# Cross-attention on one core: the scores' operand laid out by head, scores a slot later, input loads ahead of the copies

## What is computed

```python
Q = split_heads(query @ Wq + bq)          # x: (16, 512, 512)
K = split_heads(key @ Wk + bk)            # ctx: (16, 77, 512)
V = split_heads(value @ Wv + bv)
scores = einsum('bhqd,bhkd->bhqk', Q, K) / sqrt(32)
attn = softmax(scores, axis=-1)
ctx = einsum('bhqk,bhkd->bhqd', attn, V)
out = ctx.transpose(0, 2, 1, 3).reshape(B, S, 512) @ Wo + bo
return layer_norm(out + query, ln_gamma, ln_beta)
```

## Time and profile before

| | |
|---|---|
| three runs, median (lowest to highest) | 966.35 us (964.39 to 969.38) |
| the profiled execution | 968.15 us, span 966.4 us |
| mean granted TensorE clock | 0.82 |
| busy: PE, DVE, POOL, ACT | 71%, 57%, 47%, 38% of the span |
| DMA | 129.58 MB, mean 134 GB/s; packets took 50.4% of 16 engines' span |
| chain that ended last | SP's queue 33%, PE 26%, DVE 16%, DMA 7% |

### The profile page before, as it was taken

The page is one execution under the profiler, slowest core; times in us unless marked ns, Lnnn a source line. Parts: engine busy times, 40 slices in busy tenths (PEclk is TensorE's granted clock), DMA queues, the critical chain, the costliest instruction groups (busy, mean ns, idle before and its releaser), DMA issues.

```text
span 966.4 us, 11992 instructions
## 1 busy us (share of the span) xinstructions
PE 683.1 (71%) x3336; PEld 477.9 (49%) x3336; DVE 550.9 (57%) x971; ACT 367.8 (38%) x667; POOL 449.8 (47%) x399
## 2 busy tenths in 40 slices
PE   7987467677876666678776767678776767677773
PEld 6865235445554444445554444455554444455452
DVE  5343455665664546665655556666655556666635
ACT  5311332443444334443443334343443334344331
POOL 0411233554554445554544445554554445554458
PEclk9988678888887777888877777888777778888777
DMA  7643745445453555445453555445454655445432
GB/s 286 252 110 109 180 112 129 118 124 135 121 145 102 134 145 150 117 126 126 126 129 111 149 144 150 112 130 123 121 129 117 151 144 147 117 119 130 109 107 76
DMA packets 105680, 129.58 MB, mean 134 GB/s; under 512 B 49936, under 2 KB 49936, under 8 KB 105648
## 3 DMA queue, kind: packets, MB, share of 16 engines
q1 hardware_dynamic: 105648, 129.19, 50.4%
HBM read 53.94 MB, written 24.35 MB: 81 GB/s over the span
## 4 chain that ended last, share of the span: by engine, by line
SPq 33%; PE 26%; DVE 16%; issue 12%; DMA 7%; POOL 1%; ACT 0%; DVEq 0%; POOLq 0%
SPq L531 23%; PE p_o L660 13%; DVE part L813 6%; PE p_s L626 6%; SPq L517 4%; DMA z<-nmt 4%; DVE nmr L842 3%; DMA z<-ql 3%; PE p_a L612 3%; DVE ql L862 3%; SPq L468 2%; DVE y L802 2%; PE p_q L596 2%; SPq L490 1%; PE p_o L98 1%
## 5 line engine op out<-in xcount | busy, mean ns | idle before, releaser
L626 PE MATMUL p_s<-z,ks 97*77 97x512 f32 x256 | 116.9, 502 | 249.8 <-DMA z<-nmt 161.0
L718 ACT ACTIVATE prob<-p_s 77x512 f32<-77x512 f32 x256 | 144.3, 589 | 202.3 <-PE p_s L626 200.2
L870 DVE TENSOR_REDUCE nm<-p_a 128x4 f32<-128x308 f32 x256 | 118.9, 476 | 163.5 <-PE p_a L612 159.7
L972 POOL TENSOR_TENSOR cl<-cxt,ch 128x512 fp32r<-128x512 f32 x64 | 82.8, 1293 | 229.8 <-ACT ch L743 229.8
L626 PEld LDWEIGHTS p_s<-z,ks 97*77 97x77 f32 x256 | 40.7, 184 | 266.1 <-issue 207.4
L953 POOL TENSOR_TENSOR xl<-xt,xh 128x512 fp32r<-128x512 f32 x60 | 76.8, 1279 | 163.6 <-ACT xh L725 163.6
L813 DVE TRANSPOSE_TENSOR_REDUCE part<-prob 96x64 f32<-96x2048 f32 x64 | 146.9, 2295 | 9.7 <-ACT prob L718 9.7
L862 DVE SCALAR_TENSOR_TENSOR ql<-p_q,bq_col,qh 128x512 fp32r<-128x512 f32 x64 | 48.0, 749 | 172.6 <-ACT qh L733 172.5
L725 ACT CAST xh<-xt 128x512 fp32r<-128x512 f32 x60 | 36.6, 611 | 216.3 <-DMA xt<-in_x_t 216.3
L660 PE MATMUL p_o<-woh,ch 128*128 128x512 f32 x240 | 113.1, 471 | 0.3 <-DVE y L802 0.3
L660 PE MATMUL p_o<-wol,ch 128*128 128x512 f32 x240 | 111.5, 464 | 0.0
(11 more groups left out here) (123 smaller groups left out, 1038.7 us busy)
## 6 DMA issues: line engine op xcount, KB each, us to landing
z<-qh SPq DMA_DIRECT2D x256, 128.0 KB, 2.3
xt<-in_x_t SPq DMA_DIRECT2D x64, 256.0 KB, 2.8
z<-ql SPq DMA_DIRECT2D x128, 128.0 KB, 2.3
xn<-in_x SPq DMA_DIRECT2D x60, 256.0 KB, 3.3
out_dram<-y SPq DMA_DIRECT2D x60, 256.0 KB, 3.4
ks<-k_high SPq DMA_DIRECT2D x32, 154.0 KB, 3.6
cx<-in_ctx_t SPq DMA_DIRECT2D x4, 616.0 KB, 5.7
k_high<-kth SPq DMA_DIRECT2D x4, 616.0 KB, 3.5
```

Of the source, the lines that this page charges most:

```text
L626: nc.tensor.matmul(p_s[j % 2][0:S2, :], ks[0:KR, g.k // NCH % 2, h, :], z[0:KR, i, s, :], start=True, stop=True).then_inc(s_summed, 1)
L718: nc.scalar.activation(prob[0:S2, j, :], p_s[j % 2][0:S2, :], ACT.Exp, scale=SCALE).then_inc(prob_ready, 1)
L870: nc.vector.tensor_reduce(nm[:, t, HC * (g.k % 2):HC * (g.k % 2 + 1)], p_a[t % 2][:, 0:HC * S2].rearrange("p (h k) -> p h k", k=S2), AX_X, ...
L972: nc.gpsimd.tensor_tensor(cl[:, i, g.k % NCH, :], cx[:, g.k % 2, :], ch[:, i, g.k % NCH, :].bitcast(F32), ALU.subtract).then_inc(cl_ready, 1)
```

## The change

Three edits. z is indexed by head first and by chunk of the pair second, so that the two chunks of a head lie side by side: a copy writes 1024 columns in one piece, and the maxima are kept in the order head, chunk, for which `row_maxima` writes every second column of nm. LAG_SCORE goes from 2 to 3 and every later lag up by one, so the scores of chunk g come in slot g + 3 and the program of each engine has one slot more at its end. In SP's odd slot the copies stand behind kb and xt.

```diff
-LAG_SCORE = 2
-LAG_PV = 3
-LAG_OUT = 7
-LAG_NORM = 8
-LAG_SCALE = 9
-LAG_STORE = 10
+LAG_SCORE = 3
+LAG_PV = 4
+LAG_OUT = 8
+LAG_NORM = 9
+LAG_SCALE = 10
+LAG_STORE = 11
...
-        z = sb("z", [P, 2, HALF, S], F32R)
+        z = sb("z", [P, 2, HC, 2, S], F32R)
...
-                row = z[QI:KR, i, :, :].bitcast(F32).rearrange("o s (t b r) -> o s t b r", t=QT, r=DK)
+                row = z[QI:KR, i, :, :, :].bitcast(F32).rearrange("o j c (t b r) -> o (j c) t b r", t=QT, r=DK)
...
                 if g.k % 2 == 0 and g.back(2).valid(NG):
                     load_maxima(g.back(2))
-                if g.k % 2 == 1 and g.back(1).valid(NG):
-
-
-                    c = g.back(1)
-                    i = c.k // 2 % 2
-                    all_at_least(sp, (qh_ready, c.over(1, 2)), (ql_ready, c.over(1, 2)),
-                                 (s_summed, c.over(2, -1, HALF)))
-                    for part, src in enumerate((qh, qh, ql)):
-                        for j in range(HC):
-                            sp.dma_start(z[DK * part:DK * (part + 1), i, j::HC, :].bitcast(F32),
-                                         src[DK * j:DK * (j + 1), i, :, :].bitcast(F32)).then_inc(z_in[i], 16)
...
                 if g.back(LAG_LOAD_X).valid(NG):
                     load_xt(g.back(LAG_LOAD_X))
+                if g.k % 2 == 1 and g.back(1).valid(NG):
+                    c = g.back(1)
+                    i = c.k // 2 % 2
+                    all_at_least(sp, (qh_ready, c.over(1, 2)), (ql_ready, c.over(1, 2)),
+                                 (s_summed, c.over(2, -1, HALF)))
+                    for part, src in enumerate((qh, qh, ql)):
+                        for j in range(HC):
+                            sp.dma_start(z[DK * part:DK * (part + 1), i, j, :, :].bitcast(F32),
+                                         src[DK * j:DK * (j + 1), i, :, :].bitcast(F32)).then_inc(z_in[i], 16)
...
-                i, s, h = g.k // 2 % 2, HC * (g.k % 2) + j, HC * (g.k % NCH) + j
+                i, h = g.k // 2 % 2, HC * (g.k % NCH) + j
...
-                nc.tensor.matmul(p_s[j % 2][0:S2, :], ks[0:KR, g.k // NCH % 2, h, :], z[0:KR, i, s, :],
+                nc.tensor.matmul(p_s[j % 2][0:S2, :], ks[0:KR, g.k // NCH % 2, h, :], z[0:KR, i, j, g.k % 2, :],
...
-                nc.vector.tensor_reduce(nm[:, t, HC * (g.k % 2):HC * (g.k % 2 + 1)],
+                nc.vector.tensor_reduce(nm[:, t, g.k % 2:HALF:2],
```

## The result

| | before | changed |
|---|---|---|
| runs, median (lowest to highest) | 965.37 us (963.57 to 969.38) | 717.01 us (715.15 to 718.35) |
| ratio, 95% interval | | 0.7422 (0.7392 to 0.7452) |
| profiled execution, its span | 968.15, 966.4 us | 716.47, 714.7 us |
| mean granted clock | 0.82 | 0.966 |

The kernel is 248 us faster; the forecast was 672 us, 294 us faster, with a range of 652 to 722. So most of the forecast gain came, and 45 us of it didn't. Most lines have moved up by two (L626 is now L624, L813 is L811); the copies of L531 are now at L539.

The account below looks back on a forecast made before the run. SP's in-order queue, copies first, held PE idle before scores; then PE and DVE's ring would bound. 87.6 + 60 x 8.70 + 19.9 + 42.3 + 1.75 gave 673.5, less 1.8 for the median: 672 us, range 652 to 722.

Parts of the forecast that it names:

- rival 1: SP's queue becomes the bound: copies keep 0.60 us, 9.08 us a slot, 696 us in all; chance 0.16.
- S: Mean time of a slot between slots 3 and 63: 13.5 us before, forecast 8.70, from 8.4 to 8.9.
- rival 2: The DMA engines become the bound: 9.9 us a slot, 748 us; chance 0.11 with other crowding, mostly up to 9.5.
- the scores' wait and the half clock: Even slots lose 9.0 us to PE's idle stretch before scores and half clock; the change gives it back.
- the floor of 8.53 us: The ring between PE and DVE, 8.53 us in an odd slot, becomes the floor of all slots.
- the copies' 0.43 us: Issue of each z copy on SP's queue falls from 0.60 to 0.43 us; twelve then take 5.76 us.
- The ring of the forecast: SP's queue from one pair's first copy to the next pair's: 16.5 or 15.5 us, below two slots' 17.06.
- the wait from xt's issue to ACT's split, 2.79 us: Term of SP's ring: from issuing the xt load at 429.07 to ACT's split at 431.86.
- nothing waits for it: The xn load for POOL, queued behind the copies, comes earlier against ql, and nothing waits for it in slot 28.
- The rest of the sum: Slot 3 starts at 87.6 us; slot 63 to chunk 62's scores 19.9; behind them 42.3; outside the span 1.75.
- Rivals 2 to 4: 3: a wait hidden now takes half back, 811 us, 0.05; 4: slower, copies spread badly, about 1,170 us, 0.02.
- the other view, from the Trainium skill: Small pieces cost nothing extra within SBUF, so copies keep 0.60 us and the layout brings nothing.

Follow-up runs that it names:

- Experiments 1 and 2: 1: the changed kernel with the lags of before, 905.2 us; 2: the changed kernel with the copies ahead of kb and xt again, 849.77 us.
- experiment 6: The changed kernel with xt at the head of each slot's list in SP's queue and xn of odd slots ahead of the copies: 666.02 us.
- experiment 8: The changed kernel, but from the third pair on copies move only the even chunk's 512 columns, half the bytes: 717.21 us.
- experiment 9: The changed kernel, but the four ql copies of a pair read rows of the same shape from DRAM: 701.08 us.
- Experiment 10: The changed kernel, but from the third pair on the second copy of qh, four of twelve copies, is left out: 669.12 us.
- experiment 7: The changed kernel with xn of odd slots ahead of the copies and xt left where it is: 713.21 us.
- experiment 3: The changed kernel with the old layout of z, lag and order as changed: 724.74 us.
- experiment 12: The kernel of experiment 6 with xt issued from ACT's queue at the head of its slot: 669.47 us.
- experiment 4, then 5: 4: the changed kernel with xt at the head of each slot's list in SP's queue, 691.02 us; 5: with xt issued from ACT's queue, 703.61 us.

## Why the prediction was right in direction and 45 us short

*Where the result fell.* 717 us lies inside the range of 652 to 722, but the forecast's own case didn't come. By the signs that the prediction named, it is rival 1's, to which it gave 0.16: the copies stay at 0.59 us and ACT waits for xt in odd slots, which are the longer by 2 us. Rival 1's figure, 696, is 21 us short as well. That 717 is still inside is in part luck: the upper end was set by S up to 9.5, which was argued from rival 2, and rival 2 is excluded.

*Right: the scores' wait and the half clock.* Of the 249.8 us before the scores 242 are gone, and the clock followed. It held 1.00 from 300 to 650 us; from 90 to 300 us it was 0.94, where the prediction had 1.00 throughout.

*Right: lag and order are both needed.* Experiments 1 and 2 show it: 905 and 850 us against 717.

*Right: the floor of 8.53 us*, from one undisturbed slot. The changed kernel doesn't reach it in odd slots; experiment 6 comes within 0.1 us of it in the mean, and its 666 us are what the sum gives for S near 8.6.

*Wrong: the copies' 0.43 us, the term of the sum that failed.* I chose it because "source and destination differ in shape" in the slow issues. That was the wrong property. The issues that are slow are those with both ends in SBUF: the shape went (105,680 packets to 93,393) and 0.60 became 0.59; the bytes went (experiment 8) and it stayed 0.59; the source went to DRAM (experiment 9) and it became 0.42. The rows at hand were all of one kind: each fast issue had DRAM at one end, and the two slow ones hadn't. Rival 1 held that view, and its ring is the one that came. Experiment 10 shows what shorter copies are worth: with 2.5 us less of them in a pair the time is 669, near the forecast. With 7.75 us for twelve copies the two rings read above give 9.25 a slot (37.0/4). From slot 3's first p_q to slot 63's the trace gives the mean:

```profile
86.04 0.40 PE L594 MATMUL p_q<-xh,wqh 128*128 128x512 f32 x1
...
650.49 0.39 PE L594 MATMUL p_q<-xh,wqh 128*128 128x512 f32 x1
...
674.52 0.66 PE L624 MATMUL p_s<-z,ks 97*77 97x512 f32 x2
```

(650.49 - 86.04)/60 = 9.41, where I took 8.70: 60 x 0.71 = 42.6 us.

*Wrong: the wait from xt's issue to ACT's split, 2.79 us.* The ring of the forecast and that of rival 1 both have this term. It was read from the xt that goes out right behind the copies (429.07). The xt that holds the ring goes out in the even slot, behind the maxima and the ks or vb loads, and from there it took 3.51 us to the split. That could have been read before the change: the xt issued behind ks at 435.43 landed 4.1 us later, and three others in that place took 3.5 to 4.2. In the changed kernel those between 300 and 450 us took 3.4 to 3.8 behind ks and 2.6 to 3.6 behind vb. With half the bytes in the copies (experiment 8) they took 3.5 to 3.9 and 2.7 to 2.8, so behind ks the bytes of the copies are not the cause. Over the whole run the median from issue to landing is 3.5 us, where it was 2.7 before. That is some 0.7 us of a pair's ring, 0.35 a slot.

*Wrong: "nothing waits for it" about xn.* POOL waits 45.1 us for it, 28 times. Beside xt's wait that cost little (experiment 7), but with xt early it is 25 us. With copies 2.5 us a pair shorter (experiment 10) POOL waits only 4.8 us for xn, so with copies at 0.43 it would hardly have been late; at their real price it is. I should have asked of xn what I asked of xt: in which slot is it wanted, and what stands ahead of it.

*The rest of the sum.* Slot 3 started at 86.0 (forecast 87.6). From slot 63's start to the scores of chunk 62 it took 24.0 us, not 19.9: ql of 63 is late like every odd slot's, and its copies are longer. Behind them 40.2 us, not 42.3. With 1.75 outside the span: 86.0 + 564.5 + 24.0 + 40.2 + 1.75 = 716.5.

*Rivals 2 to 4.* DMA engines: experiment 8 takes their share from 0.76 to 0.55 without effect, and experiment 6, the fastest, works them harder. Its line for the same window:

```profile
300.00:500.00 200.00, 198.88 (x1116) 135.48 (x1115) 183.77 (x339) 127.41 (x233) 160.03 (x141) 1.00 0.82 208
```

Half taken back and slower: excluded by the time.

*The layout.* The prediction also had the other view, from the Trainium skill, that the copies would keep their 0.60 us, and it was the right one. "DMA: Bandwidth & Descriptors", section "Why small descriptors are slow (HBM only)" of the Trainium skill, excepts transfers within SBUF from the penalty of small pieces. The trace agrees: the queue's packets took 68.7% of 722.8 us with two pieces a row (experiment 3), 497 us, and 69.1% of 714.7 us, 494 us, with one piece and 12,288 fewer packets. It is a weak test, since the pieces here are of 2 and 4 KB. The prediction's other section there is about DMAs that GpSimd issues, while these go out from SP.

*Open.* Why is xt on ACT's queue (703.6) worse than at the head of SP's (691.0), when in experiment 12 it costs nothing to speak of? The traces show the path. In both, xn goes out 7.8 us after the first copy, but with xt on ACT's queue it lands a median of 3.6 us after its issue in place of 3.0. POOL gets to rstd later by that, and DVE, which needs rstd for nmr ahead of the next key sums, waits longer for it (us in all, times, longest; experiment 4, then 5):

```profile
DVE nmr L840 <- POOL rstd L957: 18.9, 16, 2.5
```

```profile
DVE nmr L842 <- POOL rstd L959: 28.6, 26, 2.5
```

That is 9.7 us of the 12.6 between the two times. With xn early as well the wait is 8.7 us (experiment 12). Why xn lands later stays open: the order of transfers on the DMA engines wasn't traced. Nor is it shown why a copy within SBUF takes longer to issue. Experiments 8 and 9 rest on one run each.

## What to carry to other kernels

- Before a load is moved in an in-order queue, list for each transfer the slot that wants it and what stands ahead of it. Move all of those behind the long batch, not only the one that waits today: here one gave 25 us only when the other had been moved too.
- When a price must be borrowed from another transfer, match first where both ends lie and only then shape and size; for the time until it lands, take a transfer from the same place in the queue's order. If such a price decides which ring is the longer, the other case is no minor rival.
- Read the floor from an undisturbed slot of the kernel itself. Here it was good to 0.1 us.

## What the runs showed of the hardware

- Issuing a DMA within SBUF takes SP's queue 0.59 us for 32 rows of 4 KB, and the same for 32 rows of 2 KB. With the source in DRAM and the same destination it takes 0.42. The four small copies of the maxima, also within SBUF, take 2.98 us, 0.75 each with their gaps.
- Two pieces a row in place of one add about 10 to 20 ns to an issue (eight in 5.20 us against 5.02), and 497 us of packet time a DMA engine against 494.
- The granted clock of TensorE was 1.00 from 300 to 500 us with the DMA engines busy 0.76 of the time (the changed kernel) and 0.82 (experiment 6). With a 6 us wait in every pair (experiment 1) its mean was 0.842.
